# Ids of the first chunk loaded directly, its rows taken tile by tile, and the weight turns of the first two steps placed behind the second chunk's gates

## The chip, the cores and the metric

One NeuronCore of a Trainium2 chip runs the whole kernel. The metric is the device time of one execution in microseconds. TensorE (PE in the rows) multiplies and transposes, VectorE (DVE) and ScalarE (ACT) do elementwise work, GpSimd (POOL) gathers rows and takes roots, SyncE (SP) issues the other DMAs.

## The reference

One layer of a small language model over 64 sequences of 256 token ids, with width 256 and a vocabulary of 32768. It looks rows up in an embedding table, adds a gated linear recurrence, and adds a feed-forward block with ternary weights and a low-rank correction:

```python
h = nan_to_num(take(embed_table, ids))                    # 16384 rows of 256
x = layernorm(h)
f, i, g = sigmoid(x @ Wf.T), sigmoid(x @ Wi.T), where(c >= 0, c + 0.5, sigmoid(c))   # c = x @ Wh.T
s[t] = f[t] * s[t-1] + i[t] * g[t],  s[-1] = 0.5          # over the 256 tokens of a sequence
h = h + s
x = layernorm(h)
a = bitlinear(x, w_fc) + gate * (x @ v.T @ fast_b.T @ u.T)    # ternary w_fc, 1024 x 256
h = h + bitlinear(relu(a) ** 2, w_proj)                       # ternary w_proj, 256 x 1024
```

(The reference computes the recurrence in logarithms; the lines above are the same in plain form.)

## The kernel before, in words

The 16384 tokens are cut into 32 chunks of 512 tokens, each four tiles of 128 rows (two sequences). Each engine has its own program, written out by hand; semaphores join them. An engine works strictly in the order of its program, so a wait holds up all that stands behind it.

A step n does the front of chunk n (gates, recurrence, residual) and the back of chunk n-1 (low-rank product, fc matmuls, relu, squares) and, from step 2 on, the projection of chunk n-2. Steps 0 to 4 and the last ones are unrolled; the others run in a loop. On TensorE a step is: six gate groups p = 0 to 5 of eight 128x512 matmuls (L652), with `project(n-2)`, 64 matmuls (L626), behind p = 2 and `low_rank` (L610) behind p = 4; then eight fc groups f = 0 to 7 (L696, L700), with the turn of the scanned state (`turned_rows`, L709) behind f = 4.

Before a chunk's gates can run, GpSimd gathers its four tiles with indirect DMAs (L311). VectorE bounds them (`guard`, L768, and `guard_sum`, L774, which gives `h0`) and takes statistics (`measure`, L780 and L784). GpSimd makes the reciprocal root (`root`, L321 to L329); ScalarE normalises (L391) and writes the high fp16 half (`x_high`, L398); VectorE writes the low half (`x_low`, L789); and SyncE turns each half with a DMA transpose (`turn_rows`, L257) into `x_cols`, on which the gates wait.

The weights are prepared in the same first steps. `w_raw` (Wf, Wi, Wh) is scaled by powers of two (L748 to L759), transposed (L540) and split into `w_hi` and `w_lo`. The fc weights are summed on ScalarE (L371, `abs_summed`), compared with half their scale on VectorE (`mark_below`, L837), made ternary (`make_ternary`, L842) and transposed on TensorE against the diagonal `u_diag`, which GpSimd makes (L358). The proj weights go the same way (L382, L837, L842), are turned by `turn_proj` (L596) into the PSUM tensor `y_ps` and copied out by ScalarE (`copy_proj`, L416); `project(0)` waits for all four copies. The low-rank factors pass through `low_rank_product` (L546 to L555), `scale_low_rank`, `split_low_rank`, `scale_u` and `split_u` (L881 to L891); `set_output_scales` (L898 to L910) gives the scales of the relu and of the output.

The parts of the order that matter here:

- VectorE starts with all 16384 ids (L730 to L744), then scales `w_raw`, then waits for the eight fc sums of ScalarE, marks two fc groups, and only then bounds chunk 0 as one block of 128x1024.
- ScalarE starts with the fc sums, which wait for the 1 MB load of w_fc.
- TensorE turns the state of chunk 0 at the end of step 0, ahead of step 1's gates. In step 1 it turns half the fc weights behind p = 4, and the proj weights between the fc groups f = 1, 2, 4, 5.
- ScalarE normalises `h1` of chunk 0 at the end of step 0, ahead of all gate evictions of step 1.

Of the kernel before, what the change touches and what calls it, by code (L numbers as in the profile page):

```python
# [27 lines left out]
P = 128  # L28
# [20 lines left out]
def build(nc, ids, table, wf, wi, wh, fast_b, w_fc, w_proj, u, v, gate, out):  # L49
    ctx = ExitStack()  # L50
    with ctx:
# [52 lines left out]
        ids_f = sb("ids_f", [P, 4, P])  # L104
        w_raw = sb("w_raw", [P, 6, D])
# [54 lines left out]
        ids_in, w_in, fc_in, pj_in, low_in = (sem(x) for x in ("ids_in", "w_in", "fc_in", "pj_in", "low_in"))  # L160
        blank_ready, ident_ready, consts_ready = sem("blank_ready"), sem("ident_ready"), sem("consts_ready")
# [79 lines left out]
        def _(sp):  # L241
            sp.dma_start(ids_sb[:, :], ids.rearrange("b (h p) -> (b h) p", p=P)).then_inc(ids_in, 16)
            for g, w in enumerate((wf, wi, wh)):
                sp.dma_start(w_raw[:, 2 * g:2 * g + 2, :], w.rearrange("(h p) d -> p h d", p=P)).then_inc(w_in, 16)
            sp.dma_start(v_sb[:, :], v[:, :]).then_inc(low_in, 16)
            sp.dma_start(fb_sb[:, :], fast_b[:, :]).then_inc(low_in, 16)
# [40 lines left out]
        def _(pool):  # L287
# [13 lines left out]
            def fetch_index(c, par):  # L301

                pool.tensor_copy(idx_now[:, par, :], idx_all[:, bass.ds(c * TILES, TILES)]).then_inc(idx_set, 1)
                pool.wait_ge(raw_cleared, c + 1)
                pool.wait_ge(idx_set, c + 1)
                pass_on(pool, pool_passed, c)

            def gather(c, par):

                for j in range(TILES):  # L310
                    pool.indirect_dma_start(  # L311
                        rows_raw[:, par, j, :], None, table,
                        bass.IndirectOffsetOnAxis(ap=idx_now[:, par, j:j + 1], axis=0),
                        bounds_check=V - 1, oob_is_err=False).then_inc(gathered[par], 16)
# [18 lines left out]
            clear(1, 1)  # L333
            pool.wait_ge(idx_ready, 1)
            for c in range(3):
                if c == 2:
                    root(0, 0)
                    clear(2, 0)
                fetch_index(c, c % 2)
                gather(c, c % 2)  # L340

            def step(n, h, par):
# [4 lines left out]
                if known_below(n, N - 1) and not first:  # L347
                    root(0, n + 1)
# [4 lines left out]
                if start:  # L353
                    pool.wait_ge(a_summed, 1)
                    pool.tensor_tensor(a_norm[:, :], a_ss[:, :], plus_half[:, :], ALU.pow).then_inc(a_rooted, 1)
                    root(1, 0)
# [4 lines left out]
                if first:  # L361
                    root(0, 2)
# [4 lines left out]
        def _(act):  # L367

            act.wait_ge(fc_in, 16)
            for g in range(FC):  # L370
                act.activation(fc_a[:, g, :], fc_raw[:, g, :], ACT.Abs, accum_out=fc_s[:, 0, g:g + 1])\  # L371
                    .then_inc(abs_summed, 1)


            for b in range(3):
# [3 lines left out]

            act.wait_ge(pj_in, 16)  # L380
            for k in range(KD):
                act.activation(pj_a[:, k, :], pj_raw[:, k, :], ACT.Abs, accum_out=pj_s[:, 0, k:k + 1])\  # L382
                    .then_inc(abs_summed, 1)
# [16 lines left out]
            normalise(0, 0, h0[:, 0, :, :])  # L400
            x_high(0, 0)
# [51 lines left out]
            def step(n, h, par):  # L453
# [5 lines left out]
                late = back and not first  # L459
                if late:  # L460
                    normalise(1, m, h1[:, 1 - par, :, :])
                    x_high(1, m)
                if front:
                    evict(n, 0, 0, forget, ACT.Sigmoid)
                    if start:
                        act.wait_ge(fb_turned, 1)
                        act.activation(fb_t[:, :], y_ps[0:R, 2, 32:32 + R], ACT.Copy).then_inc(fb_ready, 1)
                    evict(n, 0, 1, inp, ACT.Sigmoid)
                    if start:
                        act.wait_ge(a_ready, 1)  # L470
                        act.activation(a_sb[:, :], y_ps[0:R, 1, :], ACT.Copy).then_inc(a_copied, 1)
                        act.activation(a_sq[:, :], y_ps[0:R, 1, :], ACT.Square, accum_out=a_ss[:, :])\
                            .then_inc(a_summed, 1)
# [7 lines left out]
                if back:  # L481
                    low_high(m)
                if first:
                    for b in range(2):
                        copy_fc(b)
# [3 lines left out]
                if first:  # L489
                    for b in range(2, 4):  # L490
                        copy_fc(b)
                    for b in range(2):
                        act.wait_ge(u_turned, b + 1)
                        act.activation(low_u[:, b * 512:(b + 1) * 512], y_half[b], ACT.Copy)\
                            .then_inc(u_copied, 1)
                if back:
# [4 lines left out]
                    if first:  # L501
                        copy_proj(0)
                    clip(m, 2)
                    clip(m, 3)
                    if first:
                        copy_proj(1)
# [6 lines left out]
                    if first:  # L513
                        copy_proj(2)
# [4 lines left out]
                    if first:  # L519
                        copy_proj(3)  # L520
                    square_high(m, 3)
                    square(m, 3)
                if start:
                    normalise(1, 0, h1[:, 0, :, :])
                    x_high(1, 0)
# [4 lines left out]
        def _(pe):  # L530
# [5 lines left out]
            pe.wait_ge(w_scaled, 1)  # L536
# [5 lines left out]
            def low_rank_product(p):  # L542

                if p == 0:
                    pe.wait_ge(low_in, 64)
                    pe.transpose(y_ps[0:R, 2, 32:32 + R], fb_sb[:, :], ident[0:R, 0:R]).then_inc(fb_turned, 1)  # L546
                if p == 1:
                    pe.wait_ge(fb_ready, 1)
                    pe.matmul(y_ps[0:R, 1, :], fb_t[:, :], v_sb[:, :], start=True, stop=True).then_inc(a_ready, 1)
                if p == 5:  # L550
                    pe.wait_ge(a_scaled, 2)
                    for k in range(KD):
                        pe.transpose(y_ps[:, 2, 64 + k * R:64 + (k + 1) * R], a_sb[:, k * P:(k + 1) * P],
                                     ident[0:R, 0:R]).then_inc(a_turned, 1)
                    pe.matmul(y_ps[:, 2, 0:R], a_nb[:, :], ident[0:R, 0:R], start=True, stop=True)\  # L555
                        .then_inc(anorm_spread, 1)
# [73 lines left out]

            def step(n, h, par):
                m = n - 1
                front = known_below(n, N)
                back = not isinstance(n, int) or n > 0
                if front:
                    pe.wait_ge(x_landed[0], 32 * (n + 1))
                    for p in range(6):
# [21 lines left out]
                        if back and p == 4:  # L659
                            low_rank(n, m, True)  # L660
                        if isinstance(n, int) and n == 0:
                            low_rank_product(p)
                        if isinstance(n, int) and (n, p) == (1, 4):
                            pe.wait_ge(h1_ready, 1)
                            pe.wait_ge(fc_ready, FC)
                            pe.wait_ge(diag_ready, 1)
                            for b in range(2):
                                turn_fc(b)
# [3 lines left out]
                if isinstance(n, int) and n == 1:  # L672
# [4 lines left out]
                    turn_u()  # L677
                    pe.wait_ge(fc_copied, 4)
                    pe.wait_ge(u_copied, 2)
                    pe.wait_ge(u_ready, 2)  # L680
                for f in range(FC):
# [20 lines left out]
                    if isinstance(n, int) and n == 1 and f in (1, 2, 4, 5):  # L702
                        turn_proj((1, 2, 4, 5).index(f))
                    if front and f == 4:
# [371 lines left out]
```

## Time and profile before

| | us |
|---|---|
| three runs | 964.73, 964.75, 965.76; median 964.75 |
| the profiled execution, its own time | 964.22 |
| its span in the profile | 962.2 |
| TensorE busy | 906.2 (94%) |
| ScalarE, VectorE, GpSimd busy | 787.4, 722.7, 422.8 |

The times inside the kernel are microseconds from the start of the span. 2.0 us of the profiled execution's time lie outside its span. TensorE's clock is given as a share of 2.4 GHz: 1.00 is that level and 0.50 is 1.2 GHz.

### The profile page before, as it was taken

The page shows a single profiled execution, that of the slowest core. Times are in us where ns is not written, and L with a number is a line of the kernel's source. Part 1 is how long each engine was busy: PE and PEld are TensorE (multiplying, and loading weights), DVE is VectorE, ACT ScalarE, POOL GpSimd, SP SyncE. Part 2 cuts the span into 40 slices and gives each one's busy share as a digit, 9 for nine tenths or more (in the row PEclk, how much of TensorE's full clock was granted, in tenths as well). Part 3 has the DMA queues.
Part 4 walks back from the last instruction along what each step waited for, and adds up shares of the span by engine and source line. Part 5 has one row for each costly group of instructions (what it writes and reads, how often), then busy time and mean ns, then how long its engine had stood idle before and what let it go on. Part 6 is the DMA issues. An engine that isn't in the chain of part 4 may idle for free.

```text
span 962.2 us, 17305 instructions
## 1 busy us (share of the span) xinstructions
PE 906.2 (94%) x5313; PEld 525.9 (55%) x5313; DVE 722.7 (75%) x1250; ACT 787.4 (82%) x1159; POOL 422.8 (44%) x459
## 2 busy tenths in 40 slices
PE   1577999999999999999999999999999999999986
PEld 1233656655566566555656665566566555655654
DVE  6677687877777878787777878777878787777663
ACT  4447788998888889888888998888889888888775
POOL 6542455544445554444455544445554444433110
PEclk8788999999999999999999999999999999999999
DMA  4211232122222212222222121223212222222210
GB/s 138 55 26 26 72 71 54 43 63 56 71 71 71 69 38 58 58 60 71 71 71 60 35 68 49 71 71 71 71 45 50 61 58 70 71 67 55 34 53 35
DMA packets 161754, 57.91 MB, mean 60 GB/s; under 512 B 140358, under 2 KB 160400, under 8 KB 161728
## 3 DMA queue, kind: packets, MB, share of 16 engines
q1 hardware_dynamic: 155584, 53.38, 22.7%
q0 software_dynamic: 6144, 4.21, 1.9%
q8 instruction: 13, 0.21, 0.1%
q14 instruction: 13, 0.11, 0.0%
HBM read 19.81 MB, written 16.78 MB: 38 GB/s over the span
## 4 chain that ended last, share of the span: by engine, by line
PE 88%; ACT 4%; DVE 3%; DMA 2%; issue 1%; SPq 1%; POOL 0%; ACTq 0%; DVEq 0%
PE bank L652 33%; PE y_ps L626 22%; PE bank L696 21%; PE bank L700 5%; PE turned L709 3%; PE bank L610 3%; ACT normed L391 1%; DMA x_cols<-x_rows 1%; DMA sq<-w_fc 1%; ACT relu L438 1%; ACT x_rows L398 1%; SPq L257 0%; ACT sq L451 0%; ACT sq L371 0%; DVE hid L983 0%
## 5 line engine op out<-in xcount | busy, mean ns | idle before, releaser
L696 PE MATMUL bank<-x_cols,fc_t 128*128 128x512 f16 x1024 | 263.7, 380 | 0.7 <-issue 0.7
L652 PE MATMUL bank<-x_cols,w_hi 128*128 128x512 f16 x768 | 231.1, 383 | 22.2 <-DMA x_cols<-x_rows 19.4
L321 POOL TENSOR_SCALAR var_eps<-moments 128x4 f32<-128x4 f32 x64 | 60.5, 945 | 420.8 <-DVE moments L784 420.8
L652 PE MATMUL bank<-x_cols,w_lo 128*128 128x512 f16 x768 | 231.1, 383 | 0.0
L626 PE MATMUL y_ps<-proj_t,sq_hi 128*128 128x256 bf16 x1024 | 225.5, 273 | 2.7 <-DVE sq_lo L931 2.5
L626 PE MATMUL y_ps<-proj_t,sq_lo 128*128 128x256 bf16 x1024 | 225.5, 273 | 0.0
L438 ACT ACTIVATE relu<-bank,relu_scale 128x512 f32<-128x512 f32 x256 | 165.7, 690 | 13.7 <-PE bank L700 13.7
L311 POOL DMA_INDIRECT rows_raw<-table,idx_now x128 | 148.4, 1159 | 59.5 <-issue 31.0
L696 PEld LDWEIGHTS bank<-x_cols,fc_t 128*128 128x128 bf16 x1024 | 100.2, 98 | 114.2 <-issue 1.5
L931 DVE TENSOR_TENSOR sq_lo<-sq,sq_hi 128x1024 f16<-128x1024 f32 x128 | 150.5, 1215 | 12.1 <-ACT sq L451 12.0
L391 ACT ACTIVATE normed<-h,shift,rstd 128x256 f32<-128x256 f32 x256 | 132.7, 597 | 17.3 <-POOL shift L329 16.7
L445 ACT ACTIVATE sq_hi<-relu 128x1024 f16<-128x1024 f32 x128 | 137.1, 1071 | 1.0
L451 ACT ACTIVATE sq<-relu 128x1024 f32<-128x1024 f32 x128 | 136.7, 1068 | 0.0
L652 PEld LDWEIGHTS bank<-x_cols,w_hi 128*128 128x128 f16 x768 | 75.1, 98 | 108.0 <-DMA x_cols<-x_rows 20.3
L652 PEld LDWEIGHTS bank<-x_cols,w_lo 128*128 128x128 f16 x768 | 75.6, 98 | 92.4 <-issue 3.0
L626 PEld LDWEIGHTS y_ps<-proj_t,sq_hi 128*128 128x128 f16 x1024 | 100.1, 98 | 18.9 <-issue 2.5
L626 PEld LDWEIGHTS y_ps<-proj_t,sq_lo 128*128 128x128 f16 x1024 | 100.1, 98 | 14.8
L789 DVE TENSOR_TENSOR x_rows<-normed,x_rows 128x1024 f16<-128x1024 f32 x64 | 78.4, 1225 | 31.7 <-ACT x_rows L398 30.8
L700 PE MATMUL bank<-low,low_u 128*128 128x512 f16 x256 | 97.3, 380 | 0.6 <-DVE low L1015 0.6
L326 POOL TENSOR_TENSOR rstd<-var_eps,minus_half 128x4 f32<-128x4 f32 x64 | 91.5, 1430 | 5.3
L780 DVE BATCH_NORM_STATS2 stats<-h 128x6 f32<-128x256 f32 x256 | 89.7, 412 | 1.1
L967 DVE TENSOR_TENSOR cand<-cand_lin,cand_sig 128x512 f32<-128x512 f32 x64 | 44.3, 691 | 52.2 <-ACT cand_lin L429 52.2
(131 smaller groups left out, 942.2 us busy)
## 6 DMA issues: line engine op xcount, KB each, us to landing
out<-out_sb SPq DMA_DIRECT2D x32, 512.0 KB, 3.2
rows_raw<-table,idx_now POOLq DMA_INDIRECT x128, 2.6
x_cols<-x_rows SPq DMA_TRANSPOSE x128, 2.7
sq<-w_fc SPq DMA_DIRECT2D x1, 1024.0 KB, 7.2
pj_raw<-w_proj SPq DMA_DIRECT2D x1, 1024.0 KB, 9.4
w_raw<-wf SPq DMA_DIRECT2D x1, 256.0 KB, 2.7
w_raw<-wi SPq DMA_DIRECT2D x1, 256.0 KB, 2.9
w_raw<-wh SPq DMA_DIRECT2D x1, 256.0 KB, 3.9
```

Source lines behind the costliest of these rows:

```text
L311: pool.indirect_dma_start(rows_raw[:, par, j, :], None, table, bass.IndirectOffsetOnAxis(ap=idx_now[:, par, j:j + 1], axis=0), bounds_chec ...
L326: pool.tensor_tensor(rstd[k][:, :], var_eps[k][:, :], minus_half[:, :], ALU.pow)\
L391: act.activation(normed[k][:, j, :], rows[:, j, :], ACT.Identity, bias=shift[k][:, j:j + 1], scale=rstd[k][:, j:j + 1]).then_inc(normed_re ...
L438: act.activation(relu[:, p, f % 2, :], bank[fc_bank[f]][:, :], ACT.Relu, scale=relu_scale[:, f:f + 1]).then_inc(relu_ready, 1)
L445: act.activation(sq_hi[:, 2 * p:2 * p + 2, :], relu[:, p, :, :], ACT.Square).then_inc(sq_hi_ready, 1)
L451: act.activation(sq[:, p, :, :], relu[:, p, :, :], ACT.Square).then_inc(sq_ready, 1)
L626: ins = pe.matmul(y_ps[:, j, :], part[:, f, j * P:(j + 1) * P], proj_t[:, f, :], start=(f == 0 and j % 2 == 0 and part is sq_hi), stop=(f ...
L652: ins = pe.matmul(bank[gate_bank[p]][:, :], w[:, k, q, :], x_part(0, par, part)[:, :, k, :], start=(k == 0 and w is w_hi and part == 0), s ...
L696: pe.matmul(dst[:, :], fc_t[:, k, f * P:(f + 1) * P], x_part(1, 0, part)[:, :, k, :], start=(k == 0 and part == 0), stop=False)
L700: pe.matmul(dst[:, :], low_u[:, f * P:(f + 1) * P], low[:, :], start=False, stop=True)\
L780: dve.bn_stats(stats[k][:, j, :], rows[:, j, :]).then_inc(stats_ready[k], 1)
L931: dve.tensor_tensor(sq_lo[:, 2 * p:2 * p + 2, :], sq[:, p, :, :], sq_hi[:, 2 * p:2 * p + 2, :], ALU.subtract).then_inc(sq_lo_ready, 1)
```

## The change

**Chunk 0.** A new first DMA on SyncE's queue loads the 512 ids of chunk 0 so that they lie one row per partition, 128x4, in pieces of 4 bytes. VectorE masks these (four small operations) straight into the index tile, so that the gather of chunk 0 no longer waits for the transpose of all ids. Each of its four tiles has its own semaphore, and VectorE bounds and measures tiles 0 and 1, then 2, then 3. ScalarE and VectorE make the fp16 halves of chunk 0 two tiles at a time.

**Order at the start.** ScalarE takes the small low-rank product first, then scales `w_raw` (six instructions that were VectorE's), then sums three fc groups, splits `w_hi`, normalises chunk 0, and only then sums the other five fc groups and the proj weights. TensorE has the low-rank products ahead of the `w_raw` transposes. GpSimd issues the gather of chunk 0, waits for the low-rank sum and takes its root, issues two tiles of chunk 1, does `root(0, 0)`, and so on; the gathers of chunks 1 and 2 are cut in two around roots.

**Steps 0 to 2.** TensorE turns the state of chunk 0 behind p = 2 of step 1, and not at the end of step 0. All turns of fc, u and the scales, and `low_rank` of chunk 0 behind them, follow p = 5 of step 1. The proj turns move into step 2, behind p = 0 and p = 1. ScalarE normalises `h1` of chunk 0 behind the first six gate evictions of step 1, and copies proj at the start of step 2. VectorE's program of steps 0 and 1 is written out anew. Steps from 2 on keep their order on VectorE.

The core of the diff:

```diff
@@ sync
+            sp.dma_start(ids0_sb[:, :], ids.rearrange("b (h p) -> p (b h)", p=P)[:, 0:TILES],
+                         allow_slow_non_contiguous=True).then_inc(ids0_in, 16)
             sp.dma_start(ids_sb[:, :], ids.rearrange("b (h p) -> (b h) p", p=P)).then_inc(ids_in, 16)
@@ gpsimd
+            pool.wait_ge(idx0_ready, 1)
+            pool.wait_ge(raw_cleared, 1)
+            gather(0, 0)
+            pool.wait_ge(consts_ready, 3)
+            pool.wait_ge(a_summed, 1)
+            pool.tensor_tensor(a_norm[:, :], a_ss[:, :], plus_half[:, :], ALU.pow).then_inc(a_rooted, 1)
             pool.wait_ge(idx_ready, 1)
-            for c in range(3):
-                if c == 2:
-                    root(0, 0)
-                    clear(2, 0)
-                fetch_index(c, c % 2)
-                gather(c, c % 2)
+            fetch_index(1, 1)
+            gather(1, 1, (0, 1))
+            root(0, 0)
+            gather(1, 1, (2, 3))
+            clear(2, 0)
+            fetch_index(2, 0)
+            gather(2, 0, (0, 1))
+            root(0, 1)
+            gather(2, 0, (2, 3))
@@ scalar, the start
+            act.wait_ge(w_inv_ready, 1)
+            for g in range(6):
+                act.activation(w_raw[:, g, :], w_raw[:, g, :], ACT.Copy, scale=w_inv[:, g:g + 1]).then_inc(w_scaled, 1)
+            sum_fc(range(3))
@@ scalar, step
+                if second:
+                    copy_proj(0)
+                    copy_proj(1)
                 if late:
                     normalise(1, m, h1[:, 1 - par, :, :])
                     x_high(1, m)
                 if front:
                     evict(n, 0, 0, forget, ACT.Sigmoid)
+                    if second:
+                        copy_proj(2)
+                        copy_proj(3)
...
+                    if first:
+                        normalise(1, 0, h1[:, 0, :, :])
+                        x_high(1, 0)
@@ tensor, step
+                        if isinstance(n, int) and n == 2 and p < 2:
+                            turn_proj(2 * p)
+                            turn_proj(2 * p + 1)
+                        if first and p == 2:
+                            turn_hidden(0)
...
+                if first:
+                    pe.wait_ge(h1_ready, 1)
+                    pe.wait_ge(fc_ready, FC)
+                    pe.wait_ge(diag_ready, 1)
+                    for b in range(2):
+                        turn_fc(b)
                     turn_bound()
                     spread_proj_scale()
                     for b in range(2, 4):
                         turn_fc(b)
                     turn_u()
+                    low_rank(n, m, True)
@@ vector, ahead of step 0
+            for part in (range(2), range(2, 3), range(3, 4)):
+                for j in part:
+                    dve.wait_ge(gathered_first[j], 16)
...
+            scale_low_rank()
...
+            split_low_rank()
             guard(1, 64, 1)
             guard_sum(1, 1)
+            dve.wait_ge(h0_ready, 2)
+            measure(0, 1, h0[:, 1, :, :])
+            halve_scales(fc_s, FC, D)
+            scale_u()
@@ vector, steps 0 and 1
+                if start:
+                    mark_below(fc_raw, fc_a, fc_s, range(FC))
+                    candidate(0)
+                    weigh(0)
+                    scan(0)
+                    x_low(0, 1)
+                    guard(2, 64, 0)
+                    candidate(1)
+                    weigh(1)
+                    scan(1)
+                    residual(0, 0)
+                    make_ternary(fc_raw, fc_a, fc_s, fc_b, FC, fc_ready)
+                    guard_sum(2, 0)
+                    split_u()
+                    halve_scales(pj_s, FC + KD, HID)
+                    spread_scales()
+                    return
+                if first:
+                    candidate(0)
+                    weigh(0)
+                    scan(0)
+                    x_low(1, 0)
+                    measure_next()
+                    set_output_scales()
+                    candidate(1)
+                    weigh(1)
+                    low_half()
+                    scan(1)
+                    x_low(0, 2)
+                    residual(1, 1)
+                    guard(3, 64 * 2, 1)
+                    guard_sum(3, 1)
+                    mark_below(pj_raw, pj_a, pj_s, range(KD))
+                    make_ternary(pj_raw, pj_a, pj_s, pj_raw, KD, pj_ready)
+                    return
```

`residual` waits for `hid_turned`, adds the turned state to `h0` and measures the sum; `low_half` is the old L1015.

## Rows read from the trace of the kernel before

**Rows 1.** Busy time of each engine by stretch, and TensorE's clock:

```profile
core 0: us, PE busy (x) PEld busy (x) DVE busy (x) ACT busy (x) POOL busy (x), PEclk, DMA share, GB/s
0.00:30.50 30.50, 3.27 (x13) 2.60 (x13) 20.01 (x56) 12.52 (x30) 20.26 (x32) 0.78 0.48 129
30.50:100.00 69.50, 53.21 (x243) 25.73 (x244) 48.61 (x127) 41.42 (x68) 27.33 (x33) 0.88 0.12 28
...
106.00:962.20 856.20, 843.75 (x5004) 492.26 (x5002) 651.67 (x1066) 728.42 (x1053) 370.61 (x390) 1.00 0.25 60
...
48.00:51.00 3.00, 3.00 (x12) 2.11 (x13) 2.62 (x11) 0.00 (x0) 0.00 (x0) 0.50 0.03 5
```

**Rows 2.** The chain that ended last, up to step 0's gates (start, length, what):

```profile
4.60 7.15 DMA sq<-w_fc
11.77 3.31 ACT sq L371 x16
...
21.76 0.59 POOL shift L329
...
30.54 3.59 PE bank L652 x8
```

**Rows 3.** The same chain, steps 0 to 2:

```profile
36.62 1.85 PE bank L652 x8
...
41.74 1.06 ACT x_rows L398
...
78.59 1.11 PE y_ps L596 x4
...
89.09 2.81 DMA x_cols<-x_rows
...
98.98 6.99 PE y_ps L626 x64
```

**Rows 4.** DMA issues (us to landing), and packets from 5 to 7 us:

```profile
ids_sb<-ids SPq DMA_DIRECT2D x1, 64.0 KB, 2.0
u_raw<-u SPq DMA_DIRECT2D x1, 64.0 KB, 4.9
w_raw<-wh SPq DMA_DIRECT2D x1, 256.0 KB, 3.9
...
DMA packets 1374, 0.26 MB, mean 130 GB/s; under 512 B 1184, under 2 KB 1374, under 8 KB 1374
```

**Rows 5.** Timeline of the start (start, length, engine, line, operation):

```profile
6.05 1.75 DVE L748 TENSOR_REDUCE w_max<-w_raw 128x6 f32<-128x1536 f32 x1
7.31 1.26 POOL L311 DMA_INDIRECT rows_raw<-table,idx_now  x1 [1.01 <-POOL idx_now L303]
...
36.02 0.60 PE L549 MATMUL y_ps<-v_sb,fb_t 16*16 16x256 f32 x2
37.24 0.18 ACT L472 ACTIVATION_READ_ACCUMULATOR a_sq<-y_ps 16x1 f32 x1
```

**Rows 6.** Timeline of steps 0 and 1, the instructions that move:

```profile
30.16 3.25 DVE L842 SCALAR_TENSOR_TENSOR fc_b<-sq,fc_s 128x256 bf16<-128x256 f32 x8
49.93 1.22 DVE L1039 TENSOR_TENSOR h<-turned,h 128x1024 f32<-128x1024 f32 x1 [0.34 <-PE turned L709]
63.22 2.62 POOL L358 TENSOR_TENSOR u_diag<-ident,u_inv 128x1024 bf16<-128x1024 f32 x1 [7.30 <-DVE u_inv L872]
64.12 2.27 DVE L974 TENSOR_TENSOR value<-inp,cand 128x512 f32<-128x512 f32 x1
66.31 0.28 DVE L881 SCALAR_TENSOR_TENSOR u<-u,u_inv 128x128 f32<-128x128 f32 x1
70.46 0.29 DVE L898 TENSOR_REDUCE bound<-y_ps 128x1 f32<-128x128 f32 x1
75.05 0.69 ACT L438 ACTIVATE relu<-bank,relu_scale 128x512 f32<-128x512 f32 x1 [1.38 <-PE bank L700]
76.09 2.45 DVE L842 SCALAR_TENSOR_TENSOR pj_raw<-pj_raw,pj_s,pj_a 128x1024 f32<-128x1024 f32 x2
77.81 1.04 ACT L451 ACTIVATE sq<-relu 128x1024 f32<-128x1024 f32 x1
```

More of the change, by code:

```diff
@@ L346, in step @@
                     root(1, n - 1)
-                if known_below(n, N - 1) and not first:
+                if known_below(n, N - 1) and not start:
                     root(0, n + 1)
@@ L541, in _ @@
                 ins.then_inc(w_turned, 1)
[L542 to L556, printed above, removed]
+            turn_low_rank()
             def turn_bound():
@@ L629, in project, with turn_hidden @@
                 ins.then_inc(y_done, 1)
+            def turn_hidden(c):
+                pe.wait_ge(scanned, 4 * (c + 1))
+                wait(pe, h1_ready, c)
+                for j in range(TILES):
+                    for e in range(KD):
+                        ins = pe.transpose(turned_rows[:, j, e * P:(e + 1) * P],
+                                           hid[:, e, j * P:(j + 1) * P], ident[:, :])
+                ins.then_inc(hid_turned, 1)
             def step(n, h, par):
@@ L634, in step @@
                 back = not isinstance(n, int) or n > 0
+                first = isinstance(n, int) and n == 1
+                late = back and not first
                 if front:
@@ L984, in scan, with residual @@
                                                ALU.mult, ALU.add).then_inc(scanned, 1)
-                if late:
-                    square_low(n - 2, 0)
-                    square_low(n - 2, 1)
-                if ahead and not first:
-                    measure_next()
-                if late:
-                    square_low(n - 2, 2)
-                if late:
-                    square_low(n - 2, 3)
-                    x_low(1, m)
-                if start:
-                    mark_below(fc_raw, fc_a, fc_s, range(2, FC))
-                    make_ternary(fc_raw, fc_a, fc_s, fc_b, FC, fc_ready)
+                def residual(c, at):
+                    dve.wait_ge(hid_turned, c + 1)
+                    dve.tensor_tensor(h1[:, at, :, :], turned_rows, h0[:, at, :, :], ALU.add).then_inc(h1_ready, 1)
+                    dve.wait_ge(h1_ready, c + 1)
+                    measure(1, c, h1[:, at, :, :])
@@ L999, in step @@
+                square_low(n - 2, 0)
+                square_low(n - 2, 1)
+                if ahead:
+                    measure_next()
+                square_low(n - 2, 2)
+                square_low(n - 2, 3)
+                x_low(1, m)
                 if front:
```

245 lines of the change are left out of this document (114 added, 131 removed).

## The prediction

> **What bounds the kernel.** I read the busy times by stretch first [rows 1]. From 106 us on TensorE is busy for 843.75 of 856.2 us at its full clock, and the change leaves the order of those steps as it is. What can be won lies ahead of them: 27.2 us of idle TensorE up to 30.5, and 16.3 us more up to 100. The chain of waits tells who sets these. At the start it is the load of w_fc, the fc sums on ScalarE behind it, and then chunk 0's statistics, root (over at 22.35) and transposes: the gates start at 30.54 [rows 2]. In steps 0 to 2 it runs gates, ScalarE, transpose DMA, and late in step 1 through VectorE's ternary proj weights; step 2's gates start as the DMA lands at 91.90, and `project(0)` starts at 98.98 [rows 3]. From there TensorE has no wait worth the name. So the sum is made for one number: when does `project(0)` start, with the same work behind it. Both orders have then done the gates p = 0 to 2 of step 2, and the fc, u and proj turns.
>
> **The start.** Removed from chunk 0's path are the fc load and sums (4.60 to 15.08, [rows 2]). Left are two chains.
>
> VectorE: the new id load is 512 pieces of 4 bytes ahead of all others. Bounds for its landing are 2.0 us (all ids, 128 rows) and 4.9 us (u, 1024 pieces of 64 bytes, beside the big loads) [rows 4]. Between 5 and 7 us 1374 packets, mostly small, went at 71% busy, so 512 cost some 0.5 us: I take 2.8. The index tile is there near 4.4, the gathers are issued 1.3 us apart from about 5 (7.31 before, [rows 5]), the last lands near 13, and the moments are complete near 14.5. The Trainium skill (DMA: Bandwidth & Descriptors, Specifications) puts line rate at 512 bytes and more, with read-modify-write below. It speaks against this load; by the 4.9 us bound, taken as its price, all in the next paragraph moves by up to 2 us.
>
> GpSimd: it may not take chunk 0's root before the low-rank sum. Wh lands some 0.7 us later behind the new load, so L748 starts at 6.8 (6.05 before), takes 1.75, five small operations 0.95, the index copy 0.3: 9.85. TensorE's small product waits for that copy; product to accumulated sum takes 1.4 us (36.02 to 37.42, [rows 5]): 11.25. Then the power (0.6), the index copy, a gap of 0.9 as seen ahead of gathers, and two gathers (1.26, 0.3 and 1.0, [rows 5]): 15.65. The root takes 2.35: 18.05 against 22.35. ScalarE has finished `w_hi` by 17, one us of slack. From the root's end to the gates took 8.2 us [rows 2]. Halving does not shorten this, since SyncE needs 1.3 us per transpose issue and the low half came in time already. Gates 0 start at **26.3**, 4.2 us earlier. The fc and proj sums now stand behind it on ScalarE (4.2 us), under the transpose and cold gates: free.
>
> **Step 0 to step 1's gates.** p = 0 at the low clock takes 3.6 us, p = 1 and 2 1.8 each [rows 2, 3], over at 33.6 (26.3 + 3.6 + 3.7) with the small products gone. The evictions, `normalise` and `x_high` took 4.3 us from there (38.49 to 42.80, [rows 3]): 37.9; issue of two transposes and landing 4.1: gates 1 at **42.0** (49.68 before, behind the state's turn). The lead is 7.7 us at its largest.
>
> **The new wait.** VectorE has scanned by about 43 and stands at `residual(0, 0)` until TensorE has turned the state behind p = 2: p = 0 cold 3.6, two groups 3.45, the turn 0.9: 50.0. VectorE idles some 7 us, where it had waited 0.34 [rows 6]. Queued behind are, in order: residual and statistics 3.0 (L1039 on); ternary fc 3.25; `guard_sum` 1.2; `split_u` 2.15; proj scales 0.8; candidate and weight 1.45; scan 1.2; `x_low` 1.2; statistics 1.8; output scales 1.95 (durations: L842, L881, L898 in [rows 6], and one instruction each of the page's groups). That is 18.0: **68.0**. TensorE waits for each: fc turns until 56.3, scales until 60.4, the last u turn until 68.0. Then u turn 0.65, low-rank at the low clock 1.85, ScalarE's copy 0.65, VectorE's low half 0.7, last matmul and first relu: the first relu is at 72.35 (75.05 before, [rows 6]). The lead has shrunk to 2.7 us.
>
> It grows once more, as the proj turns and copies are gone from here: relu 0, relu 1 and both squares took 3.8 us (75.05 to 78.85, [rows 6]), then two relus 1.2, `normalise` and `x_high` 3.15, so chunk 2's high half is ready at 80.5, and the gates of step 2 start 4.2 us later: **84.75** against 91.94.
>
> **The end of the lead.** On VectorE the ternary proj weights now stand behind `x_low(0, 2)` and the residual: from 80.5: 1.25, residual and statistics 3.0, guards 1.9, marks 1.4, ternary 2.45 [rows 6]: **90.5**. They were ready at 78.54. TensorE finishes p = 0 at 88.35 and waits 2.15 us for them. Then four transposes took 1.11 after such a wait [rows 3], copy 0.6, the second turn's copy 0.6, and now ScalarE's order decides: `normalise` and `x_high` of chunk 1 (3.15), one eviction 0.6, copies 2 and 3 (1.2) come ahead of `project(0)`: 90.5 + 1.1 + 1.2 + 3.15 + 0.6 + 1.2 = **97.8**. TensorE's own way (turns 2.8, p = 1 and 2 3.5) is over at 96.8. Against 98.98 that is 1.2 us.
>
> Profiled time 964.22 - 1.2 = 963.0 (span 961.0); that execution is 0.5 under the median, so on the median **963.6**. A change under 0.2% (1.93 us) cannot be told from none.
>
> **A collision.** GpSimd's `u_diag` takes 2.62 us, and VectorE's product beside it took 2.27 instead of 0.69 [rows 6]. It moves to about 39.1, just when `x_low(0, 1)` (37.9 to 39.15) ends; it then hits `guard(2)` and `weigh(1)`, which have 4 us of cover. Were GpSimd a us ahead, `x_low` would stand behind it, at up to 2.6 us on the path: bounds 0 and 2.6, I take 0. The Trainium skill (SBUF — State Buffer, Who interferes with whom) says that whichever starts first keeps the shared port for the whole instruction; by that rule the outcome hangs on this order alone, and the row agrees.
>
> **Rivals.**
> - *The clock does not fall in the shorter wait ahead of gates 1.* After about 4 us of idleness the turn and first gates ran at 0.50 [rows 1]. The wait is now 3.4 us; if it stays up, 1.7 us are saved: 961.9. Other waits of 2.5 us did both.
> - *The lead of step 2's gates is kept* (7.2 us, 957.6), if the ternary proj weights were there by 88.3. VectorE's queue speaks against it; its terms are all rows.
> - *The change doesn't do what it says:* chunk 0's root comes no earlier than 22.3, as the weights land late behind the small pieces, and the low-rank wait holds GpSimd. The start gives nothing and the rest of the chain costs its 3.0: 967.8. It turns slower once that root ends after 21.2. Against it: 4.9 us for u are the worst row, which explains only part.
> - *Slower by the clock:* step 2 has p = 0, a wait, turns. If 3.6 us of work do not lift TensorE's clock for good, p = 1, p = 2 and the turns run at the low level: 90.5 + 2.2 + 3.5 + 2.2 + 3.5 = 101.9, 2.9 us late: 967.7. It decides from 100.9 on. Against it: each cold stretch before ended within about 3.5 us of work.
>
> **Chances.** The forecast 0.52, its own range 961.5 to 965.3 (start 1 us either way, clock 1.7 us, part of the id bound); clock kept 0.20; lead kept 0.05; start not earlier 0.08; clock low 0.07; collision on the path (+1.4, 966.2) 0.08. Low end: the clock case with a us more. High end: the collision. 960.8 to 966.2 leaves out the lead kept, the late start and the low clock, 0.20. Faster: 0.16 + 0.17 + 0.05 = 0.38; slower: 0.08 + 0.07 + 0.03 = 0.18; same 0.44.
>
> **What would show it.** Chunk 0's root ending at 18, gates at 26.3, 42.0 and 84.75, `project(0)` at 97.8; VectorE idle some 7 us ahead of the first residual, released by TensorE; ternary proj weights at 90.5 with TensorE waiting for them; then a tail of the same length. Wrong would be: gates 0 later than 28, no wait of VectorE, or a tail behind `project(0)` of another length.

## The result and the profile after

The changed kernel takes 970.63 us (median of 7 runs, 966.56 to 972.3) against 966.1 us for the kernel before on the same chip (7 runs, 964.73 to 968.43): a ratio of 1.0044, 95% interval 1.0026 to 1.0062. It is slower by more than the 0.2% that can be told from no change, and it lies outside the predicted range. The profiled execution took 970.55 us with a span of 968.7 us; before it was 964.22 and 962.2. That execution of the kernel before lies 1.9 us under its median of 966.1, so the spans differ by 6.5 us where the medians differ by 4.5. Of all runs below two were slow ones at a far lower granted clock, one of e5 (1231 us) and one of the kernel before beside it (1098 us), and no median or ratio here contains them.

The prediction was made for one number, the start of `project(0)`, so that is read first. The chain that ended last in the changed kernel (start, length, engine, what), to be held against [rows 2] and [rows 3]:

```profile
23.98 3.80 DMA x_cols<-x_rows
27.82 7.74 PE bank L688 x24
...
39.92 3.58 DVE x_rows L815
43.52 2.80 DMA x_cols<-x_rows
46.37 6.99 PE bank L688 x24
53.36 0.89 PE turned L661 x8
54.27 1.24 DVE h L1043
...
71.27 0.49 DVE proj_scale L936
...
85.03 1.23 DVE x_rows L815
...
93.77 1.29 DVE pj_raw L868
95.10 1.97 PE y_ps L620 x8
97.06 3.41 PE bank L688 x8
100.48 1.15 PE y_ps L620 x8
101.63 1.73 PE bank L688 x8
103.36 6.99 PE y_ps L650 x64
...
941.50 1.89 PE bank L634 x4
```

The change does what it says at the start: step 0's gates begin at 27.82, 2.7 us earlier than in [rows 2]. At `project(0)` nothing is left of that: 103.36 against 98.98, 4.4 us later. What stands in between is a chain in which VectorE's queue has grown. In the kernel before it ran through gates, ScalarE and the transpose DMA as far as `x_low(1, 0)`, and from there through VectorE's queue for 19.4 us, up to the ternary proj weights at 78.54; the prediction's account of that chain names only the end of this stretch. Two of its rows, from the kernel before:

```profile
59.14 1.23 DVE x_rows L789
...
71.85 0.04 DVE proj_scale L910
```

In the changed kernel VectorE's queue holds 27.5 us of the chain: 17.5 from the residual at 54.27 to the output scales, ready at 71.77, and 10.0 from `x_low(0, 2)` at 85.03 to the ternary proj weights, ready at 95.06.

The windows of the changed kernel (columns as in [rows 1]) show the rest of the loss:

```profile
27.80:103.36 75.56, 53.34 (x227) 26.44 (x228) 53.34 (x127) 42.15 (x66) 28.78 (x34) 0.82 0.13 30
...
940.00:942.00 2.00, 0.50 (x2) 0.23 (x3) 0.99 (x1) 0.00 (x0) 0.00 (x0) 0.65 0.57 132
942.00:944.00 2.00, 2.00 (x6) 0.66 (x5) 0.00 (x0) 0.57 (x1) 0.00 (x0) 0.50 0.72 253
```

Between the first gates and `project(0)` the mean granted clock is 0.82, where [rows 1] has 0.88 for about the same work. And the tail is not of the same length: from `project(0)` to the end of the span it takes 968.7 - 103.36 = 865.34 us, against 962.2 - 98.98 = 863.22 before. Ahead of the last chunk's low-rank product (the row at 941.50) TensorE waits 3.3 us for a transpose, and its clock is at 0.50 behind it, the lower level of the two (1.2 GHz); in the kernel before it waits the same 3.3 us there, and the clock is at 1.00 behind it. So the 6.5 us by which the span grew are 4.4 ahead of `project(0)` and 2.1 at the far end.

Three rows of the timeline show where the first stretch lost (start, length, engine, line, operation, form; in brackets the idle time ahead and who ended it):

```profile
39.92 3.57 DVE L815 TENSOR_TENSOR x_rows<-normed,x_rows 128x1024 f16<-128x1024 f32 x1 [0.32 <-ACT x_rows L417]
...
40.50 1.90 POOL L372 TENSOR_TENSOR u_diag<-ident,u_inv 128x1024 bf16<-128x1024 f32 x1
...
54.27 1.23 DVE L1043 TENSOR_TENSOR h<-turned,h 128x1024 f32<-128x1024 f32 x1 [7.54 <-PE turned L661]
...
95.10 1.97 PE L620 MATMUL y_ps<-ident,pj_raw 128*128 128x128 f32 x8 [3.91 <-DVE pj_raw L868]
```

`x_low(0, 1)` takes 3.57 us beside GpSimd's `u_diag`; the same line takes 1.23 us in its next instance. VectorE stands 7.54 us ahead of the first residual, where [rows 6] had 0.34. And TensorE stands 3.91 us ahead of the proj turns.

### The profile page after: what moved, and what is told of

Its sections match the earlier page's. It is cut to its first block, busy times and chain, and to the rows that moved or that the text cites. A ratio compares the mean times of both kernels' runs of the same rounds, so it can differ in the third digit from the quotient of the medians.

```text
span 968.7 us, 17303 instructions
## 1 busy us (share of the span) xinstructions
PE 912.1 (94%) x5313; PEld 529.5 (55%) x5313; DVE 724.1 (75%) x1249; ACT 791.4 (82%) x1166; POOL 421.3 (43%) x458
## 4 chain that ended last, share of the span: by engine, by line
PE 89%; DVE 4%; ACT 3%; DMA 2%; issue 2%; SPq 0%; ACTq 0%; POOL 0%; POOLq 0%; DVEq 0%
PE bank L688 34%; PE y_ps L650 22%; PE bank L735 21%; PE bank L739 5%; PE bank L634 3%; PE turned L661 3%; DMA x_cols<-x_rows 1%; ACT relu L468 1%; ACT normed L410 1%; DVE x_rows L815 1%; DMA rows_raw<-table,idx_now 1%; DVE stats L806 0%; ACT sq L481 0%; ACT sq_hi L475 0%; ACT x_rows L417 0%
## 5 line engine op out<-in xcount | busy, mean ns | idle before, releaser
L1037 DVE TENSOR_TENSOR_SCAN hid<-forget,value 128x256 f32<-128x256 f32 x128 | 81.6, 680 | 1.2
```

## The experiments

All are edits of the changed kernel. Nine kernels ran, in three groups; within a group they shared a chip and its runs of the kernel before (medians 966.12, 967.22 and 966.86 us). The table gives the results, with the start of step 0's gates and of `project(0)` in each profiled execution, and the length from there to the span's end. Seven executions have one and the same start (the changed kernel, its repeat, e1 to e4 and e8); their gates 0 lie between 27.64 and 29.30 us, with the second gather of chunk 0 landing at 11.69 to 13.58. That much is scatter, so the stretch from gates 0 to `project(0)` tells more of an edit than either time alone.

| kernel | us, median (runs) | ratio to before, 95% | gates 0 | project(0) | behind it |
|---|---|---|---|---|---|
| changed, again | 971.40 (10) | 1.0039 (1.0015 to 1.0062) | 28.51 | 103.68 | 865.4 |
| e1, u_diag early | 967.08 (12) | 1.0018 (1.0005 to 1.0032) | 29.30 | 102.22 | 863.2 |
| e2, turn early | 966.42 (12) | 1.0002 (0.9986 to 1.0018) | 28.86 | 99.42 | 865.4 |
| e3, ternary first | 964.70 (12) | 0.9974 (0.9955 to 0.9993) | 29.17 | 99.48 | 864.6 |
| e4 = e1 + e2 + e3 | 958.55 (6) | 0.9919 (0.9898 to 0.9939) | 27.64 | 90.50 | 864.2 |
| e5, w_proj late | 970.39 (11) | 1.0022 (1.0000 to 1.0045) | 27.32 | 103.36 | 865.4 |
| e6 = e4 + e5 | 957.93 (6) | 0.9910 (0.9890 to 0.9930) | 26.67 | 91.70 | 864.4 |
| e7, statistics whole | 969.78 (12) | 1.0036 (1.0019 to 1.0054) | 30.02 | 101.15 | 863.3 |
| e8, start alone | 961.25 (7) | 0.9943 (0.9923 to 0.9963) | 28.43 | 94.02 | 865.3 |

**The changed kernel again**, with no edit, as the level for the others.

> The changed kernel once more, as the yardstick for the three beside it. My theory is that the loss arises ahead of project(0) and the rest is of the same length: project(0) starts near 103.4 and the time is 4 to 5 us over the kernel before, near 970.6. The rival, that part of the loss sits in the steps behind, is told by the length from project(0)'s start to the span's end: 863.2 before and 865.3 in the profile of the changed kernel; if the 2.1 us come from TensorE's clock at the last low-rank product, they come and go between executions.

971.40 us repeats the result. Its ten runs fall into two clusters, three at 964.42 to 964.94 and seven at 971.12 to 972.38 us. TensorE's granted clock, averaged over the whole run, is 0.989 to 0.990 in the three and 0.971 to 0.982 in the seven. So the clock has a part in it, but its mean does not give the time: 971.12 us goes with 0.982 and 972.38 with 0.971. Where runs fall into two clusters the median can land in either; by the means (969.6 us here) e1 gains 2.2 us, e2 3.6 and e3 5.7, each give or take some 2.5 to 2.8, an estimate from the scatter of the runs. For e1 that is not clear of no gain at all.

**e1: the collision taken away.** GpSimd makes `u_diag` ahead of clearing and gathering chunk 3:

```
                 if known_below(n, N - 1) and not start:
                     root(0, n + 1)
-                if known_below(n, N - 3):
-                    clear(n + 3, 1 - par)
-                    fetch_index(n + 3, 1 - par)
-                    gather(n + 3, 1 - par)
                 if start:
                     ...
                         .then_inc(diag_ready, 1)
+                if known_below(n, N - 3):
+                    clear(n + 3, 1 - par)
+                    fetch_index(n + 3, 1 - par)
+                    gather(n + 3, 1 - par)
+                if start:
                     root(1, 0)
```

> u_diag moves ahead of the clearing and gather of chunk 3 on GpSimd. Theory C (the collision is on the path): x_low(0, 1) takes 1.2 us instead of 3.57, gates 1 start at 44.0 instead of 46.37, and project(0) 2.35 us earlier, at 101.0: near 968.3. Rival Q (VectorE's order behind its wait sets the end): gates 1 start earlier just the same, and as VectorE's wait ends with them all behind it moves as well, so Q gives the same here; what would tell against both is a project(0) that stays at 103.4, held by something else, such as the gather of chunk 3 coming 2 us later or TensorE's clock.

Its chain:

```profile
29.30 7.79 PE bank L689 x24
...
41.46 1.24 DVE x_rows L816
42.73 3.13 DMA x_cols<-x_rows
45.91 8.01 PE bank L689 x24
53.91 0.89 PE turned L662 x8
```

`x_low(0, 1)` is back at 1.24 us. From gates 0 to gates 1 it takes 16.6 us (18.3 in the repeat of the changed kernel), but then the three groups of gates 1 take 8.01 us instead of 7.0, the clock staying low for longer, so the residual starts at 54.82, no earlier than the repeat's 54.66. In this profile the collision alone hence gave almost nothing there; what is gained by `project(0)` (1.5 us) comes mostly from step 2's turns at a better clock, and 2.2 us from a tail without the low clock. The stretch from gates 0 to `project(0)` is 2.3 us shorter than in the repeat (72.92 against 75.17). The median is 4.3 us below the changed kernel's, the mean 2.2, and the fastest run (966.12) is above the fastest of the repeat (964.42). The collision costs 2.35 us where it stands, but what reaches the end depends on the clock behind it.

**e2: the new wait of VectorE taken away.** TensorE turns the state ahead of step 1's gates, as in the kernel before:

```
+                if first:
+                    turn_hidden(0)
                 if front:
                     pe.wait_ge(x_landed[0], 32 * (n + 1))
...
-                        if first and p == 2:
-                            turn_hidden(0)
```

> The turn of chunk 0's state goes back in front of step 1's gates. Theory Q (VectorE's queue behind the residual sets the end): the scan ends at 46.7, the turn at the low clock at 48.8, the residual starts there and not at 54.27, the gates 2.4 us later than 46.37, at 48.8; the output scales are ready near 66.3 instead of 71.77 and project(0) starts near 98: near 965. Rival (the gates set the end, and the delay of 2.4 us passes on): project(0) near 105.8, near 973.

```profile
42.50 2.29 DVE cand L1021
...
46.87 1.97 PE turned L661 x8
48.84 10.57 PE bank L690 x40
...
67.34 0.50 DVE proj_scale L936
...
91.16 1.97 PE y_ps L620 x8
...
99.42 5.68 PE y_ps L650 x52
```

The turn costs 1.97 us ahead of the gates at the low clock, and the residual starts at 48.88 instead of 54.66. The output scales are ready at 67.83 instead of 72.16, the ternary weights 4.3 us earlier, and `project(0)` starts at 99.42. So the wait for the turn was on the path with all of VectorE's queue behind it: 4.3 us at `project(0)` and 5.0 us in the median. A collision is still in this: `u_diag` (42.31 to 44.22) misses `x_low(0, 1)` here and meets the candidate product, which takes 2.28 us instead of 0.69 and holds up the scan, the turn and, as the turn now stands ahead of them, the gates.

**e3: the other end of VectorE's queue.** The proj marks and ternary weights go ahead of `x_low(0, 2)`, the residual and the guards:

```
                     scan(1)
+                    mark_below(pj_raw, pj_a, pj_s, range(KD))
+                    make_ternary(pj_raw, pj_a, pj_s, pj_raw, KD, pj_ready)
                     x_low(0, 2)
                     residual(1, 1)
                     guard(3, 64 * 2, 1)
                     guard_sum(3, 1)
-                    mark_below(pj_raw, pj_a, pj_s, range(KD))
-                    make_ternary(pj_raw, pj_a, pj_s, pj_raw, KD, pj_ready)
```

> The marks and the ternary proj weights move ahead of x_low(0, 2), into the 7.7 us in which VectorE waits for it. Theory Q: they are ready near 81.3 instead of 95.05, TensorE's wait of 3.9 us behind p = 0 is gone, and project(0) starts near 99.2: near 966.4, about the kernel before. Rival (ScalarE's order decides, copies behind normalise): the copies of proj cannot start before its squares end at 93, and normalise, an eviction and two copies follow: project(0) not before 99, so by both near 99; if project(0) moves by less than 3 us, ScalarE or the clock holds it and Q's share is small.

In the changed kernel VectorE stood idle for 7.73 us just ahead of `x_low(0, 2)`, with this work queued behind it:

```profile
85.03 1.23 DVE L815 TENSOR_TENSOR x_rows<-normed,x_rows 128x1024 f16<-128x1024 f32 x1 [7.73 <-ACT x_rows L417]
```

The ternary block fits into that hole. `project(0)` starts at 99.48, although gates 0, the slow `x_low(0, 1)` (3.58 us here too) and the output scales (72.20) are all as late as in the changed kernel or later. In the median it is the largest single gain, 6.7 us (5.7 by the means), and the edit alone turns the change from slower to just faster than the kernel before.

What holds `project(0)` now is ScalarE. TensorE waits 0.55 us for the last two proj copies, which stand behind the squares, `normalise` and an eviction:

```profile
98.45 0.98 ACT proj_t L446 x2
```

So the rival of this expectation holds too, and as both had said about 99, the time alone would not have told them apart.

**e4: the three together.**

> The three edits of the single runs together: u_diag before the gather of chunk 3, the turn of chunk 0's state before step 1's gates, the ternary proj weights before x_low(0, 2). Theory: the collision (2.35 us), VectorE's late start behind the residual and the late proj weights are separate costs in one chain, so the gains add up as far as the next thing allows. From gates 0 near 28.5: scan over near 45, turn cold until 47, output scales near 64.7, first relu near 71, chunk 2's high half near 79, gates 2 near 83, project(0) near 93: near 960. Rival: they overlap (each took the same slack), and the sum is no better than the best single one, project(0) near 99, 965.

```profile
43.86 1.73 PE turned L662 x8
45.59 9.69 PE bank L691 x40
...
63.21 0.50 DVE proj_scale L937
...
80.78 2.73 PE bank L691 x8
83.51 1.72 PE y_ps L621 x8
...
90.50 7.16 PE y_ps L651 x64
```

958.55 us, 8.7 us below the kernel before. `project(0)` starts at 90.50, 13.2 us ahead of the changed kernel's repeat; the three alone had given 1.5, 4.3 and 4.2 at that place, 9.9 together. Most of the surplus is the scatter of the start: counted from gates 0 the three give 2.3, 4.6 and 4.9 us, 11.7 together, and e4 gives 12.3. The costs are separate and add up. In e4 TensorE no longer stands before the proj turns: p = 0 runs straight into them (80.78 + 2.73 = 83.51), where the changed kernel had its wait and the low clock behind it. Ahead of `project(0)` it waits 0.94 us for ScalarE's copies.

**e5: the start made faster.** SyncE waits for chunk 0's four gathers before it loads w_proj:

```
             sp.dma_start(fc_raw[:, :, :], w_fc.rearrange("(g p) d -> p g d", p=P)).then_inc(fc_in, 16)
+            for landed in gathered_first:
+                sp.wait_ge(landed, 16)
             sp.dma_start(pj_raw[:, :, :], w_proj.rearrange("(g p) f -> p g f", p=P)).then_inc(pj_in, 16)
```

> The changed kernel with SyncE waiting for the four gathers of chunk 0 before it issues the 1 MB load of w_proj. Theory D (the big loads hold the first gathers: they took 5.3 to 7.2 us to land against 2.6 later): they land within 3 to 4 us, chunk 0's moments are complete near 14 instead of 17.1 to 18.4, GpSimd's two gathers (until 15.8) then hold the root, and gates 0 start near 26.5 instead of 27.8 to 29.3: 1.3 to 2.5 us earlier all the way, near 969. Rival: the gathers are slow because w_fc, w_raw and the small pieces are in front of them as well, so the landing moves by less than a us. The proj sums on ScalarE must not come late: they run at 24.5, the load would land near 19.

The gathers landed 4.6, 5.1, 3.9 and 2.8 us after their issue instead of 5.3, 5.5, 6.3 and 5.6, and gates 0 began at 27.32. But `project(0)` stands at 103.36, to the hundredth where it stood, and the median is that of the changed kernel. The start gained 0.5 us and not the 1.3 to 2.5 of the theory: VectorE begins as the second gather lands, at 11.55 instead of 11.91, and is then busy to 16.57 whatever the later gathers do. Behind it gates 0 take 8.05 us and gates 1 7.48, 0.3 and 0.5 more than in the changed kernel. **e6** puts the same edit into e4:

> e4_three and the late w_proj load together. If theory D holds, 1.3 to 2.5 us under e4_three; if not, the same as it.

957.93 us, not to be told from e4 (958.55), and the lowest median of all. Gates 0 start at 26.67, 1.0 us before e4's, and `project(0)` at 91.70, 1.2 us after it: gates 0 take 8.16 us instead of 6.76, and the 40 matmuls behind the turn 10.28 instead of 9.69.

**e7: chunk 0's statistics as one block** instead of by tiles:

```
-            for part in (range(2), range(2, 3), range(3, 4)):
+            for part in (range(4),):
```

> The changed kernel with one edit: chunk 0's statistics, reciprocals and low-rank terms are done as one block for the four tiles, after the fourth gather, instead of tile by tile as the gathers land. Theory (the tiles' statistics cost 5.1 us in all but start before the last gather, the block costs the 3.8 us of the kernel before and starts when the last gather is in, near 14.6 to 15.5): the moments are ready at 18.4 to 19.3 instead of 17.1, gates 0 starts 1 to 2 us later, near 29 to 30, and the time is 0 to 1.5 us more than the changed kernel's. Rival: the pieces' own cost eats the whole lead, gates 0 starts within 0.5 us of the changed kernel's 27.8 to 28.5, and the time is the same. In both, residual(0,0), the slow x_low(0,1) and the late ternary block stay as they are.

The timeline and chain of this kernel:

```profile
15.61 0.69 DVE L942 TENSOR_SCALAR rows_fin<-rows_raw 128x1024 f32<-128x1024 f32 x1 [6.24 <-DMA rows_raw<-table,idx_now]
```

```profile
30.02 6.91 PE bank L688 x24
...
45.80 7.04 PE bank L688 x24
...
94.05 1.47 PE y_ps L620 x8
95.52 3.03 PE bank L688 x8
98.55 0.87 PE y_ps L620 x8
99.42 1.73 PE bank L688 x8
101.15 6.99 PE y_ps L650 x64
...
939.32 1.05 PE bank L634 x4
```

The block starts at 15.61 and the moments are there at 19.43; by tiles they were there at 17.09. Gates 0 start 2.2 us later than in the changed kernel, about as the theory said, and 0.7 to 2.4 later than in the seven executions with the start by tiles. The rest of that theory fell: gates 1 start at 45.80, 0.57 us *earlier*, and the time is not longer (969.78 against 971.40 and 970.63). Of the 2.2 us, 0.8 come back as gates 0 run at a better clock (6.91 us instead of 7.74), and the collision, which both theories had kept, is gone: `x_low(0, 1)` starts at 41.30 and is done in 1.23 us before `u_diag` begins at 43.41 (it meets the candidate product instead, 2.27 us, off the path). In this execution, one of the faster of its twelve, the clock was also up for part of step 2's turns and at the far end, which is worth 7.10 us instead of 8.26 up to `project(0)` and 2.1 us behind it. So the pieces buy some 1.5 us at gates 0, against the mean of those seven (28.53), and in this change's order no gain from them can be told in the time.

**e8: the start alone.** The direct ids, the gathers and the statistics by tiles stay; every engine's order in steps 0 to 2 is put back to that of the kernel before (state turned before step 1's gates, fc turns behind its p = 4 group, proj turns and copies between the fc groups of step 1, `make_ternary` of fc ahead of the first scan, `u_diag` behind `root(1, 0)`). Its core on VectorE:

```
                 if start:
                     mark_below(fc_raw, fc_a, fc_s, range(FC))
+                    make_ternary(fc_raw, fc_a, fc_s, fc_b, FC, fc_ready)
                     candidate(0)
...
                     residual(0, 0)
-                    make_ternary(fc_raw, fc_a, fc_s, fc_b, FC, fc_ready)
                     guard_sum(2, 0)
-                    split_u()
+                    x_low(1, 0)
```

> The start of the changed kernel (direct ids, gather and statistics by tiles, the order ahead of step 0) with the old order of steps 0 to 2 on all engines. Theory: the start alone brings gates 0 to 28.5 +- 0.7 instead of 30.54 and the old chain carries these 2 us to project(0), near 97 instead of 98.98, or a little less, as small products have gone from step 0: near 964, 2 us under the kernel before; the new order of steps 0 to 2 is then what costs the changed kernel 6 us. Rival: the old order gives the start's gain back as well (a fixed wait on VectorE or a load), project(0) near 99.

```profile
28.43 7.79 PE bank L692 x24
...
45.68 1.98 PE turned L665 x8
47.68 1.24 DVE h L1044
...
56.92 1.24 DVE x_rows L816
...
66.77 0.04 DVE proj_scale L937
...
86.98 7.04 PE bank L692 x24
94.02 6.99 PE y_ps L654 x64
```

961.25 us, 0.57% faster than the kernel before. `project(0)` starts at 94.02: 5.0 us ahead of [rows 3] and 9.3 ahead of the changed kernel. That is 3 us better than the theory, which had carried 2 us from gates 0 to the end. They are carried: 2.1 us at gates 0, 2.2 at `x_low(1, 0)` (56.92 against 59.14). But the output scales are ready 5.1 us earlier (66.80 against 71.89), as `scale_u`, 2.4 us of VectorE's queue from 60.75 on in the kernel before, now stands ahead of step 0, and the value product no longer runs beside `u_diag` (0.69 us instead of 2.27). No run parts this move of small work from the new loads and gathers. With that said, the experiment splits the change in two: all that stands ahead of step 0 is worth 5 us at `project(0)` (6.0 in the median), and the new order of steps 0 to 2 costs 9.3 there. Step 2's three groups of gates run as one stretch of 7.04 us here; cut by turns and a wait they take 103.36 - 89.29 = 14.1 us in the changed kernel, 3.1 of them the turns themselves.

## Why the prediction was wrong

The sum gave 97.8 for `project(0)`, and 103.36 was measured, 5.6 us later. By the prediction's own steps (each term is its measured length less the one I gave):

| step | predicted | measured | off |
|---|---|---|---|
| gates 0 start | 26.3 | 27.82 | +1.5 |
| gates 0 to `x_high` done | 11.6 | 12.1 | +0.5 |
| `x_low` and landing, to gates 1 | 4.1 | 6.5 | +2.4 |
| gates 1 to the residual | 8.0 | 7.9 | -0.1 |
| VectorE's queue, residual to output scales | 18.0 | 17.5 | -0.5 |
| to the first relu | 4.35 | 5.0 | +0.7 |
| to chunk 2's high half and the ternary weights | 18.15 | 18.3 | +0.1 |
| ternary weights to `project(0)` | 7.3 | 8.3 | +1.0 |
| the tail | 863.2 | 865.3 | +2.1 |

The first eight rows add up to the 5.6 us. The 963.6 forecast for the median started from 964.75, the median of three runs; over seven the kernel before has 966.1, so 1.35 of the 7.0 us between 963.6 and 970.63 belong to that level and to no term.

**What was right.** VectorE's new wait ahead of `residual(0, 0)` is there (7.54 us for "some 7"), released by TensorE. The 18.0 us queued behind it, added from single rows, measured 17.5. The ternary weights being late and TensorE waiting for them was right as well, and e2 and e3 show that these two waits, not the start, decide. The direction came out wrong although the mechanism had been seen: the predicted net gain of 1.2 us was a difference of terms of 4 to 18 us, and all the misses but two small ones went the same way.

**The start** (+1.5). The id load was not the cause: its 512 small pieces landed 2.2 us after issue, within the 2.8 that I took. The Trainium skill (DMA: Bandwidth & Descriptors, Specifications) speaks of less than line rate below 512 bytes; at this size hardly a cost of it shows: all ids took 2.0 us in [rows 4]. The mis-sized term is "the last lands near 13, and the moments are complete near 14.5". The gathers were issued at 4.85 to 9.02 us and took 5.3 to 6.3 us each, ending at 14.6; those of the kernel before were issued from 7.31 and landed by about the same time. e5 shows in part why: with w_proj held back they take 2.8 to 5.1 us. What bound was not the last of them, though: VectorE began as the second was in, at 11.91, and its statistics took 5.1 us in pieces with no further wait of note, so that the moments were there at 17.09, 2.6 us after the 14.5 of the sum. The sum let GpSimd hold the root until 15.65; it began at 17.18, and that is the 1.5. The low-rank work on GpSimd, on which I let the root wait, was over before and did not bind.

**A collision** (+2.4). I priced it at nothing, gave it a chance of 0.08 and 1.4 us, and rested on the order of two instructions that were a us apart in my sum. Measured, they overlap in the changed kernel, its repeat, e3 and e5, and miss each other in e2 and e7, where `u_diag` meets the candidate product instead, though up to that point both queues of e2 are those of the changed kernel. A term that hangs on one us of timing between two engines should have stood at its middle, and not at its better bound.

**The end of the lead** (+1.0). I let ScalarE's order decide, with "TensorE's own way" over 1.0 us before it. In the changed kernel TensorE's own way ended last; ScalarE's order did in e3, e4 and e6. The turns took 1.97 and 1.15 us and p = 1 took 3.41 us at the low clock. That is the rival "slower by the clock" in part: p = 1 ran cold, p = 2 did not. I had it at 101.9 with a chance of 0.07, starting from the ternary weights at 90.5; counted from the measured 95.06 it would have been 106.5, and came at 103.36.

**The tail** (+2.1). "A tail of the same length" took the tail for fixed. In the profiled executions it is 863.2 to 865.4 us, and goes with TensorE's clock at the last transpose: the last low-rank product takes 1.05 us in the kernel before, e1 and e7, and 1.89 in the changed kernel, its repeat, e2 to e6 and e8, behind a wait of 3.3 to 3.7 us in all of them. The table shows that it follows neither the order of steps 0 to 2 nor the start. What sets it was not found; as it comes and goes between kernels of the same order, part of the 2.1 us may lie in which execution was profiled. Nor is it shown that the two clusters of times are made of this and of step 2's clock alone: those two account for 1.2 + 2.1 us between e7's profile and that of the changed kernel, and the medians of the clusters lie 6.9 us apart.

**The rivals.** "The lead of step 2's gates is kept" did not happen, but e3 shows that one move in VectorE's queue is what it wanted. "The change doesn't do what it says" fell: the root ends at 19.14. The clock ahead of gates 1 fell, as forecast.

## What to carry to other kernels

When an engine's queue is reordered, look at where it stands idle and what is queued behind that point: here 3.7 us of ternary work stood behind a hole of 7.7 us, and the move of two lines was worth as much as the whole new start (5.7 us each by the means). An earlier start is worth something only if the waits behind it move too; add up the queue behind each new wait before counting a lead as kept. And test the parts of a change apart: this one held a gain of 5 us and a loss of 9.3.

## What the runs showed of the hardware

- **A VectorE instruction that started first was still held by GpSimd.** In the changed kernel `x_low(0, 1)` starts at 39.92 and `u_diag` at 40.50; `u_diag` takes 1.90 us to 42.40 and `x_low` ends at 43.49, 1.09 us after it, about the whole of its own 1.23. The repeat and e3 give the same 3.57 us with `u_diag` 0.57 and 0.56 us behind; in e5, with `u_diag` 0.08 us ahead, it is 2.92. In all four `x_low` ends 1.09 or 1.10 us after `u_diag` ends, whichever started first. The Trainium skill (SBUF — State Buffer, Who interferes with whom) says that two-input VectorE instructions contend with GpSimd's reads, which these rows agree with, and, in its line on VectorE's 2-port modes, that "whoever issues first gets the shared pair for the whole instruction". By the starts in the trace that does not hold here. Nor does the row of [rows 6] bear it out as the prediction says: `u_diag` started there at 63.22, the candidate product at 63.40, and the product took its 0.68 us while `u_diag` took 2.62 instead of 1.90. Spans on GpSimd are rough, and whether `u_diag` really began earlier can't be told from them. In the other direction a gather whose issue started 0.20 us into `x_low` took 1.89 us instead of 1.00 (e2), so each can hold the other.
- **Gathers issued earlier beside the big loads do not land as much earlier.** Issued 2.5 us earlier than before, they took 5.3 to 6.3 us, where the same four took 3.5 to 5.8 in the kernel before, and the last landed at 14.6 instead of 15.0. The median over all 128 gathers of the changed kernel is 2.7 us.
- **Behind waits of 2 to 4 us the clock fell in some executions and not in others.** Ahead of the last low-rank product TensorE waits 3.3 us both in the kernel before and in the changed kernel, and runs it at 1.00 in the one and at 0.50 in the other. At the start of step 2 of the changed kernel it waits 3.90 us for the DMA and runs its next group at the full level, then waits 3.91 us and runs 3.41 us of p = 1 at the low one; in e7 the group behind the first of these waits is the cold one and the second wait, 2.46 us, costs less. Cutting TensorE's first work of a step into pieces with a wait between them thus cost more here than the wait itself.
